# Four chained attention and Fourier blocks: 23 unread TensorE products near the end are taken out

## What is computed

```python
x = _L0_conv_ref(x, w_conv, w_gap)   # softmax(x^T x), a projection, pooled gap weights, + x
x = _L1_conv_ref(x, q_w, ..., gamma) # q, k, v projections, 1024 x 1024 softmax, gamma*out + x
x = _L2_conv_ref(x, wa, ..., gama)   # softmax over 8 neighbours, channel softmax, elu, mix with x
x = _L3_conv_ref(x, w_in, w_out)     # project to 16 maps, 2-D FFT, angular energy, gain, inverse FFT, + x
```

## Time and profile before

| what | us |
|---|---|
| median of 3 runs | 278.42 (278.32 to 278.46) |
| the profiled execution, its own time | 278.63 |
| its span, first to last instruction | 276.8 |
| TensorE busy | 264.9 (96%) |
| ScalarE busy | 184.7 (67%) |
| VectorE busy | 174.3 (63%) |

### The profile page before, as it was taken

One profiled execution on the slowest core, in us unless ns is written; L12 is line 12 of the kernel. 1 busy time (PEld: TensorE's weight loads), 2 busy tenths in 40 slices (PEclk: granted clock), 3 DMA queues, 4 the chain that ended last, 5 costly groups with the idle time before them and its releaser, 6 DMA issues.

```text
span 276.8 us, 4058 instructions
## 1 busy us (share of the span) xinstructions
PE 264.9 (96%) x1328; PEld 157.1 (57%) x1331; DVE 174.3 (63%) x297; ACT 184.7 (67%) x355; POOL 63.3 (23%) x97
## 2 busy tenths in 40 slices
PE   7999999999999999999999999988999998899993
PEld 2864666457655665563667535844545546664573
DVE  4686769687645743276776978777325247646773
ACT  1584477887887667665787577988846758647430
POOL 2016018300400002537821300110003607500000
PEclk9999999999999999999999999999999999999999
DMA  5990000000000010000000000000000000000026
GB/s 170 281 305 3 0 0 4 23 26 26 4 0 0 0 54 2 0 1 1 3 0 1 0 2 1 4 1 0 0 1 0 2 0 4 1 1 2 1 78 227
DMA packets 4573, 8.52 MB, mean 31 GB/s; under 512 B 1250, under 2 KB 2018, under 8 KB 4554
## 3 DMA queue, kind: packets, MB, share of 16 engines
q1 hardware_dynamic: 4554, 8.27, 9.1%
HBM read 5.60 MB, written 2.10 MB: 28 GB/s over the span
## 4 chain that ended last, share of the span: by engine, by line
PE 87%; ACT 4%; DVE 3%; DMA 2%; issue 1%; SPq 0%; DVEq 0%; ACTq 0%
PE psum L366 84%; DMA qs<-row 2%; DMA xin<-in_x 1%; PE psum L491 1%; DVE nmax L890 1%; DVE xl L852 1%; SPq L354 0%; ACT L748 0%; ACT L742 0%; ACT e L661 0%; DVE x L871 0%; ACT qs L676 0%; DVEq L199 0%; PE psum L467 0%; ACT x2T L698 0%
## 5 line engine op out<-in xcount | busy, mean ns | idle before, releaser
L366 PE MATMUL psum<-e,v 128*128 128x512 f32 x128 | 60.0, 593 | 0.0
L890 DVE TENSOR_REDUCE nmax<-psum 128x1 f32<-128x1024 f32 x32 | 38.5, 1221 | 19.6 <-PE psum L366 19.6
L661 ACT ACTIVATE e<-psum,nmax 128x1024 f32<-128x1024 f32 x32 | 35.7, 1115 | 18.0 <-issue 12.7
L861 DVE TENSOR_REDUCE nmax<-psum 128x1 f32<-128x1024 f32 x32 | 39.0, 1221 | 11.5 <-PE psum L366 10.9
L694 ACT ACTIVATE e<-psum 128x1024 f32<-128x1024 f32 x32 | 32.2, 1024 | 14.1 <-PE psum L366 13.6
L684 ACT ACTIVATE psum<-psum,nmax 128x1024 f32<-128x1024 f32 x32 | 34.9, 1091 | 8.5 <-DVE nmax L890 8.5
L366 PEld LDWEIGHTS psum<-e,v 128*128 128x128 f32 x128 | 23.7, 189 | 18.9 <-issue 15.9
L1051 POOL CAST qs<-qs 32x512 fp32r<-32x512 f32 x16 | 9.7, 606 | 102.9 <-ACT qs L676 102.1
L366 PE MATMUL psum<-qs,ks 96*128 96x512 f32 (+1 forms) x96 | 30.1, 415 | 2.4 <-DMA qs<-row 2.0
L366 PE MATMUL psum<-ks,qs 96*128 96x512 f32 (+1 forms) x96 | 31.1, 428 | 1.0 <-ACT e L694 0.7
L366 PE MATMUL psum<-e,v0n 128*64 128x512 f32 x128 | 30.9, 605 | 0.0
(11 more groups left out here) (174 smaller groups left out, 409.8 us busy)
## 6 DMA issues: line engine op xcount, KB each, us to landing
out<-xin SPq DMA_DIRECT2D x8, 256.0 KB, 2.1
xin<-in_x SPq DMA_DIRECT2D x3, 512.0 KB, 6.2
twist<-in_twist_in SPq DMA_DIRECT2D x1, 768.0 KB, 8.6
zz<-in_region_in SPq DMA_DIRECT2D x2, 360.0 KB, 6.7
xin<-in_x SPq DMA_DIRECT2D x2, 256.0 KB, 2.7
untwist<-in_untwist_in SPq DMA_DIRECT2D x1, 512.0 KB, 8.2
e<-in_near_in SPq DMA_DIRECT2D x1, 272.0 KB, 8.8
rw<-in_rows_w SPq DMA_DIRECT2D x1, 256.0 KB, 2.7
```

The costliest lines, as they stand in the source:

```text
L366: return nc.tensor.matmul(o, lhsT, rhs, start=start, stop=stop, skip_group_check=skip)
L661: inc(go(e0[:, E0_AT[b, i], :], t[:, :], ACT.Exp, bias=nmax0[z][:, i:i + 1], accum_out=sum0[z][:, i:i + 1]), "e0_ready", b)
L861: inc(vec.tensor_reduce(nmax0[z][:, i:i + 1], t[:, :], AX.X, ALU.max, negate=True), "nmax0_ready", b)
L890: inc(vec.tensor_reduce(nmax1[z][:, i:i + 1], t[:, :], AX.X, ALU.max, negate=True), "nmax1_ready", b)
```

## The change

The 23 warm steps near the end are taken out of TensorE's list; the nine at the start stay. Nothing else is edited. For six of the steps that stay, the earlier holder of the bank was a warm step; it is now the last real step that held it:

| step | earlier holder before | after |
|---|---|---|
| energy.0@3 | warm.20 | nearT.3.0 |
| s2.3@4 | warm.19 | nearT.3.1 |
| selT.0@5 | warm.24 | nearT.3.1 |
| energy.1@6 | warm.28 | joinc.3 |
| coefT.0@7 | warm.30 | joinc.3 |
| i2.1@3 | warm.29 | energy.0 |

```diff
     "joinc.3.0@6 nearT.3.0@2 xproj.2.0@0 nearT.3.1@4 joina.3.0 xturn.2.0@0 joinb.3.0 s1.2.0@0 joinb.3.1 s2.2.0@0 "
-    "warm.0.9@5 warm.0.10@4 warm.0.11@3 warm.0.12@5 warm.0.13@4 warm.0.14@3 warm.0.15@5 warm.0.16@4 warm.0.17@3 "
-    "warm.0.18@5 warm.0.19@4 warm.0.20@3 warm.0.21@7 xproj.3.0@2 warm.0.22@7 warm.0.23@6 warm.0.24@5 xturn.3.0@1 "
-    "energy.0.0@3 s1.3.0@2 warm.0.25@7 warm.0.26@6 s2.3.0@4 warm.0.27@7 warm.0.28@6 warm.0.29@3 selT.0.0@5 "
-    "warm.0.30@7 region.0.0@5 energy.1.0@6 coefT.0.0@7 coefT.1.0@5 i1.0.0@0 i1.1.0@1 i2.0.0@0 coefT.2.0@2 "
+    ""
+    "xproj.3.0@2 xturn.3.0@1 "
+    "energy.0.0@3 s1.3.0@2 s2.3.0@4 selT.0.0@5 "
+    "region.0.0@5 energy.1.0@6 coefT.0.0@7 coefT.1.0@5 i1.0.0@0 i1.1.0@1 i2.0.0@0 coefT.2.0@2 "
     "i2.1.0@3 wout.0.0@6 selT.1.0@5 wout.0.1 region.1.0@4 wout.1.0@0 i1.2.0@3 wout.1.1 coefT.3.0@2 i2.2.0@3 "
-    "i1.3.0@2 wout.2.0@4 wout.2.1 i2.3.0@6 warm.0.31@7 wout.3.0@0 wout.3.1")
+    "i1.3.0@2 wout.2.0@4 wout.2.1 i2.3.0@6 wout.3.0@0 wout.3.1")
```

## The result

The changed kernel took 283.52 us in the median of four runs (282.33 to 284.08), the kernel before beside it 278.44 us; the ratio is 1.016, with a 95% interval of 1.0103 to 1.0217. The forecast was 279.5 us in a range of 278.1 to 281.8 us: the direction was right, the size far too small, and the time lies outside the range. The profiled execution took 283.98 us, with a span of 282.2 us against 276.8.

What follows compares the result with a forecast made beforehand. TensorE, 96% busy, was taken to bound the kernel. A clock fall costing 1.0 us, plus 0.2 us at s2.3, less 0.10 us gained, made +1.1 us; set to the 278.42 us median, 279.5 us, range 278.1 to 281.8.

Steps and rivals of the forecast that it cites:

- The clock falls behind the pause: After s2.2, TensorE 15% busy over 4.4 us loses its full clock; 6 in 10.
- The removed products gain 0.10 us at region.0: Between selT's cast and region.0, a streaming unread product delays the start; removing it gains 0.10 us on the chain.
- What each group costs at half speed: From xproj.3 on, streamed time doubles: xturn 0.2, energy 0.8, s1 0.54, s2 0.75 us more.
- s2.3's lateness costs 0.3 us at most: s1.3 and s2.3 slow by 1.29 us against 0.94 us free before selT.0; 0.3 us gets through if both are slow.
- the +3.0 us bound: Upper bound of the slower case: clock low to about 263.4 us, 1.0 + 0.3 + 0.8 + 0.1 + 0.8.
- So I expect it back near 258 us: Over 3 us of unbroken xturn, energy.0 and s1.3 raise the clock again, leaving +1.1 us.
- the sign given for a longer fall: i1's 16 records, 1.07 us before, would take near 2 us, or wout's would lengthen as well.
- The holding rival: After s2.2 the clock stays full over the pause; only the 0.10 us gain remains, 278.3 us; chance 0.34.

Runs made afterwards that it cites:

- the ten kept: Against the kernel before, the 13 unread products behind s2.2 out, the ten later ones left in; 279.94 us, ratio 1.0026.
- the block cut to four: Against the kernel with two products added in the row-DMA wait: 13 products behind s2.2 cut to four, those ahead of region.0 and wout.3 out; 279.08 us.
- the block and the three out: Against the kernel with two products added in the row-DMA wait: 13 products behind s2.2 and three behind xproj.3 out, seven later ones kept; 280.55 us.
- the DMA wait filled: Against the changed kernel, two products added in the row-DMA wait near 180 us, ahead of scoreT.2.0, all 23 still out; 282.11 us, ratio 1.0088.
- the ten out: Against the kernel before, only the last ten unread products out, the 13 behind s2.2 kept; 279.94 us, ratio 1.0047.
- four at the start: Against the kernel before, the 13 products behind s2.2 cut to four at the pause's start, ten later ones kept; 279.81 us, ratio 1.0007.

## Why the prediction was wrong, by its own steps

- **The clock falls behind the pause, at 6 in 10.** Right. It fell in the profiles of all the kernels in which the block was out, and with the ten kept in at least seven of ten runs, the profiled one and six at 279.6 to 280.05 us with mean clocks of 0.993 and 0.994; in two it held.
- **The removed products gain 0.10 us at region.0.** Wrong. The 0.15 us stayed without the product. That xproj.3 would start earlier was right (0.05 us behind x3 in the changed kernel) and worth nothing, as said. Its end stayed under ScalarE's table load at the low level too, by 0.09 us (256.63 against xrow at 256.72 us), near the 0.06 us computed.
- **What each group costs at half speed.** Right to a few hundredths: xturn 0.24 us for 0.2, energy.0 0.75 for 0.8, s1 0.52 for 0.54, s2 0.70 for 0.75, energy.1 0.74 for 0.8, i1 0.87 for about 0.9 streamed.
- **s2.3's lateness costs 0.3 us at most.** The term was mis-sized. selT.0 came 0.21 us later than energy.0's copy explains, which fits, but a further 0.38 us came through VectorE's list, where selT's cast stands behind pw.3: 0.59 us in all. With coefT, i1 and i2 at 1.02 us for the 0.9 us summed, this is what parts the +3.0 us bound (clock low to i1) from the measured 3.39.
- **"So I expect it back near 258 us."** This is the step that failed. Over 3 us of unbroken work at the low level were set against the 2.7 us of unread products that raised the clock at the start, and the length of that work was taken to decide the return. The work was there, 3.49 us of xturn.3, energy.0 and s1.3 without a break, and the clock did not return behind it but at 268.95 us, behind i1. The same steps did raise it where the fall came just as they began, in the profiles of the block cut to four (1.16 us in all) and of the block and the three out (1.25 us): there the predicted course is what happened. What the step left out is that the return depends on where the fall lies against the work, that this differs between executions, and that a return missed here is followed by the two waits, so that the next one comes only behind i1. The term sized at 1.0 to 1.1 us measured 3.39 in the changed kernel's profile and 2.74 in that with the DMA wait filled.
- **The range.** Its upper end came from the clock staying low up to i2, +3.0 us. That is where it came back, and the sign given for a longer fall, i1 near 2 us, was seen (1.94 us). So the edit's own 3.39 us, on top of 278.42, reach just the end of the range, 281.8 us; with the DMA wait filled the median was 282.11 us. What took the time far out of the range is the next point.
- **The rest of the distance.** 283.52 − 278.44 is 5.1 us, 3.4 of them the edit's by the profile. Most of the others are in executions that also fell behind the row DMA at 183.6 us. That is seen in the profiled one; for the other three it is argued from the run with that wait filled, of which none reached 283 us. The kernel before does so in about three runs of ten, but the three runs that the prediction had were all of the low group, and nothing in its profile showed a fall. No term of the sum stood for it.
- **The holding rival.** The rule of the Trainium skill's page "TensorE: Matmul & The Clock Gate" (section "Why this matters for your kernels"), by which such a pause is short enough, does not hold here: the measured falls came with an idle piece of 2.75 us, and even behind waits of 1.03 us (183.6 us) and 0.95 us (262.8 us). The same page of the Trainium skill (section "A second HAM failure mode: psum-queue depth-cycling") has small idles between groups of matmuls move the clock; the kernel with the ten out agrees in so far as it fell behind small waits, once in its profile and not over and over.

What stays open: why the same work raises the clock in one execution and not in another, and whether the kind of a product plays a part. That 3 rows are worth less than 128 rests on one profile and ten runs. That narrow stationary tiles are worth less was not tried alone, and the two returns over energy.0 speak against it.

## What to carry to other kernels

Products that nobody reads can be load-bearing: in a wait they cost nothing on the path here and hold TensorE's clock, so before they are taken out each stretch is to be asked twice, whether the clock falls there, and what in the work that follows would bring it back. Once it has fallen they are not free: ahead of xturn.3 they cost 0.53 to 0.66 us at half speed. A fall at the head of a tail of small steps with waits between them can last through much of it, here for 10.2 us in one execution and 13.6 us in another, and for 3.4 us where part of the products stayed, so its cost is better forecast as a spread than from the one return that the length of the work suggests. Where single runs of a kernel lie in two groups, look for a wait of about 1 us in the middle of dense work: with two wide products in it none of twelve runs was in the upper group here, and two of twelve in each of two kernels built on that.

## What the runs showed of the hardware that was not expected

- Busy share does not order the falls: the clock fell behind 2.35 of 3.40 us busy (changed kernel, 183.6 us), 2.30 of 3.40 (ten out, 262.8 us) and 2.43 of 3.40 (four at the start, 243.0 us), and held over 2.28 of 3.40 us and over 1.36 of 3.30 us (four at the start). The first three end at the fall; the two that held were laid where the work was thinnest, so the comparison is rough, and some records can be missing.
- The clock falls over the same instructions in some executions and not in others: at the row DMA near 180 us in about three of ten.
- The same 3.5 us of unbroken small products at the low level raised the clock in one execution (block and three out, fall at 255.60 us, back at 259.0) and not in another (changed kernel, fall at 255.30 us, the three steps from 257.15 to 260.64, back at 268.95).
- What a fall costs varies with how long the clock stays low: in the last stretch 3.4 us in seven profiles (0.97 to 1.4 us of time), 10.2 and 13.6 us in two (2.74 and 3.39 us).
- Four products of 3 rows take as long as of 128 rows (374 against 379 ns) and the clock fell behind them, as with no products.
